# One scan and one product by C over both channel blocks of a step, and all pairs summed by TensorE

## The chip, the cores and the metric

One Trainium2 chip, one core of it. The metric is the device time of one execution in microseconds (us). The engines are called PE (TensorE), DVE (VectorE), ACT (ScalarE), POOL (GpSimd) and SP (SyncE, which issues the DMAs). SBUF is the on-chip memory; PSUM is the accumulator memory, here eight banks of 512 fp32 columns over 128 partitions.

## The reference

A decoder layer on 2048 tokens of 256 channels: layer norm and a Mamba block with its feed-forward part, then cross attention, then a mixture of experts. The change lies in the Mamba block's selective scan, for 512 channels d and 16 states n:

```
def step(h, inp):
    d_t, u_t, b_t, c_t = inp
    dA = jnp.exp(d_t[..., None] * A)
    h = dA * h + (d_t * u_t)[..., None] * b_t[:, None, :]
    y = jnp.einsum('bdn,bn->bd', h, c_t)
    return (h, y)
```

d_t is the step size (a softplus), u_t the channel's input, b_t and c_t come from a projection of u. A is minus the exponential of a weight, so every decay dA lies between 0 and 1. The sequence is one of 2048 steps of time.

## The kernel before

The time axis is cut into four chunks (`NC`) of 512 columns. The 512 channels are four blocks of 128 partitions, taken two at a time: half p = 0 holds blocks 0 and 1, half 1 holds blocks 2 and 3 (`DP` = 2 blocks). A **step** w is one chunk, one half and one state n: 32 steps a chunk (`NU`), 128 in all (`NW_ALL`). A step's work:

- ACT, `decays`: two exponentials of 128x512 into two PSUM banks (2, 3 for even w, 4, 5 for odd w), x = 0 and x = 1. The banks come free when step w - 2 is done with them.
- POOL, `scan_input`: `dbu` = `du` times B, 128x1024, into a ring of three buffers (`DR`), ahead of DVE.
- DVE, `scan` (L864), once for each block x: the recurrence along 512 columns, in place in PSUM, started from the block's column of `carry`. `times_c` (L875), once for each block: the states times C into `hs`, a ring of six. `carry_over` (L882): the last column of both blocks, a 128x2 copy, for the next chunk.
- PE, `add_states`: an identity matmul of 128x512 for each block and state, which sums the states in PSUM banks 0 and 1. An fp32 matmul of 512 columns is two records in the trace. Two steps make a pair j. For the pairs in `SUMMED` (15 of the 64, every fourth but the last) POOL adds the two states first (`add_pair`, L437), and PE sums one state.
- SP, `load_b` and `load_c`: rows of B and C for two steps, broadcast to 128 partitions, two buffers each.

The order of each engine is written out by hand. DVE's loop is

```
for w in range(NW_ALL):
    scan(w, 0)
    if w >= 1:
        times_c(w - 1, 1)
    between(w // NU, w % NU)
    scan(w, 1)
    times_c(w, 0)
    carry_over(w)
```

so that between a scan and its own product another scan stands. `between` (L930 to L988) holds the side work of the neighbouring chunks at a given step i of the chunk: the convolution of the next chunk (steps 9 to 12), the step sizes (`step_rounded` to `step_channels`, steps 6 to 9 and 24 to 28), the gate of the finished half (`gated`, L890, steps 3 and 19), the residuals (`first_residual`, L895; `second_residual`, L911, at step 2 of chunks 2 and 3) and the norms. ACT and PE have their side work at given steps too: ACT the step projection's softplus (steps 4, 5, 22, 23), SiLU (14, 16) and GELU (24, 26, 28, 30); PE the projections, `hidden` (23 to 29) and `ffn_out` (30, 31 and the next chunk's 0, 1). PE's `skip` (L1306) opens the sum of a half and waits for DVE's gate of the half before. The functions of ACT change the activation table: exponential, logarithm, SiLU and GELU each load their own, copies none.

All sharing is by semaphores. A function that waits for its own engine's semaphore waits until the earlier instruction has written.

## Time and profile before

| | |
|---|---|
| median of 3 runs | 1638.37 us (1637.38 to 1647.46) |
| profiled execution: span | 1636.5 us |
| median less that span | 1.9 us |
| busy: PE, DVE, ACT, POOL | 1336.6, 797.4, 904.6, 402.9 us |
| first and last scan start at | 49.7 and 659.4 us |

The span runs from the first to the last instruction of one profiled execution, the only figure that the page gives for that execution. What lies around it in a timed run is of the size of the third line. An engine's busy time is a sum over stages: DVE is busy nearly throughout up to about 660 us, PE and ACT more after it.

### The profile page before, as it was taken

The page shows a single profiled execution, that of the slowest core. Times are in us where ns is not written, and L with a number is a line of the kernel's source. Part 1 is how long each engine was busy: PE and PEld are TensorE (multiplying, and loading weights), DVE is VectorE, ACT ScalarE, POOL GpSimd, SP SyncE. Part 2 cuts the span into 40 slices and gives each one's busy share as a digit, 9 for nine tenths or more (in the row PEclk, how much of TensorE's full clock was granted, in tenths as well). Part 3 has the DMA queues.
Part 4 walks back from the last instruction along what each step waited for, and adds up shares of the span by engine and source line. Part 5 has one row for each costly group of instructions (what it writes and reads, how often), then busy time and mean ns, then how long its engine had stood idle before and what let it go on. Part 6 is the DMA issues. An engine that isn't in the chain of part 4 may idle for free.

```text
span 1636.5 us, 15496 instructions
## 1 busy us (share of the span) xinstructions
PE 1336.6 (82%) x5511; PEld 628.7 (38%) x5511; DVE 797.4 (49%) x1213; ACT 904.6 (55%) x1164; POOL 402.9 (25%) x177
## 2 busy tenths in 40 slices
PE   6477566887598748896735999999999988979999
PEld 2122123343334324653521223223223234568887
DVE  3899989989998899216520002001011016461011
ACT  3536444654466436122435997998998944751310
POOL 0637655654455466015030000000000001000000
PEclk9588787999789878998756999999999988989999
DMA  5323332332243233102994000000000000011701
GB/s 184 118 78 129 129 115 86 122 116 77 82 138 116 77 128 116 45 8 49 102 112 39 1 1 1 1 1 0 0 0 0 0 0 1 1 52 35 325 14 39
DMA packets 35633, 107.96 MB, mean 66 GB/s; under 512 B 3650, under 2 KB 14146, under 8 KB 32915
## 3 DMA queue, kind: packets, MB, share of 16 engines
q1 hardware_dynamic: 35572, 107.19, 23.7%
q8 instruction: 34, 0.56, 0.1%
q14 instruction: 27, 0.22, 0.1%
HBM read 93.60 MB, written 2.36 MB: 59 GB/s over the span
## 4 chain that ended last, share of the span: by engine, by line
PE 47%; DVE 24%; ACT 13%; issue 8%; DMA 5%; SPq 1%; POOL 1%; DVEq 0%; ACTq 0%; POOLq 0%
DVE ps L864 13%; PE ps L1558 10%; PE ps L1543 9%; ACT arena L706 6%; PE ps L1362 4%; PE ps L1667 4%; DMA arena<-arena 4%; PE ps L1708 3%; PE ps L1317 3%; DVE arena L875 2%; PE ps L1685 2%; PE ps L1696 2%; PE ps L1248 2%; SPq L377 1%; PE ps L1588 1%
## 5 line engine op out<-in xcount | busy, mean ns | idle before, releaser
L706 ACT ACTIVATE arena<-ps,bound 128x1024 f32<-128x1024 f32 (+1 forms) x416 | 421.1, 1215 | 26.7 <-PE ps L1543 26.7
L431 POOL TENSOR_TENSOR arena<-arena 128x1024 f32<-128x1024 f32 x128 | 300.7, 2353 | 262.0 <-DVE ps L864 218.1
L864 DVE TENSOR_TENSOR_SCAN ps<-ps,arena 128x512 f32<-128x512 f32 x256 | 327.3, 1279 | 18.1 <-ACT ps L567 13.7
L1317 PE MATMUL ps<-arena,ident 128*128 128x512 f32 x452 | 245.1, 683 | 106.1 <-POOL arena L437 66.1
L567 ACT ACTIVATE ps<-arena 128x512 f32<-128x512 f32 x256 | 173.1, 689 | 269.1 <-DVE arena L882 175.5
L1543 PE MATMUL ps<-arena 97*128 (+3 forms) x832 | 218.9, 385 | 22.8 <-issue 20.7
L1558 PE MATMUL ps<-arena 128*32 128x512 f32 (+1 forms) x1664 | 222.8, 607 | 1.1 <-ACT arena L706 0.9
L1317 PEld LDWEIGHTS ps<-arena,ident 128*128 128x128 f32 x452 | 91.5, 214 | 243.3 <-issue 89.0
L1141 DVE COPY arena<-ps 128x512 f32<-128x512 f32 x16 | 11.1, 691 | 355.8 <-PE ps L1558 355.8
L419 POOL TENSOR_TENSOR rstd<-ve,mhalf 128x4 f32<-128x4 f32 (+3 forms) x18 | 23.5, 1308 | 625.0 <-DVE ve L1166 469.9
L875 DVE TENSOR_TENSOR arena<-ps,arena 128x512 f32<-128x512 f32 x256 | 171.4, 669 | 0.0
L1543 PEld LDWEIGHTS ps<-arena 97*128 97x128 bf16 (+1 forms) x832 | 67.5, 99 | 227.0 <-ACT arena L706 140.6
L1248 PE MATMUL ps<-ident,arena 128*128 128x128 f32 x392 | 58.7, 291 | 40.4 <-DVE arena L1051 13.7
L1248 PEld LDWEIGHTS ps<-ident,arena 128*128 128x128 f32 x392 | 45.1, 147 | 76.0 <-issue 57.5
L1362 PE MATMUL ps<-arena 128*128 128x256 f32 x256 | 62.5, 400 | 12.1 <-ACT arena L583 12.1
L1558 PEld LDWEIGHTS ps<-arena 128*32 128x32 f32 (+1 forms) x1664 | 32.9, 108 | 95.5 <-ACT arena L706 78.3
L1262 PE MATMUL ps<-arena 128*128 128x512 f32 x128 | 62.9, 639 | 4.1 <-DVE arena L895 2.4
L1353 PE MATMUL ps<-arena 128*128 128x512 f32 x128 | 59.9, 615 | 5.5 <-ACT arena L583 4.8
L1667 PE MATMUL ps<-arena 128*128 128x257 f32 x256 | 58.6, 393 | 2.5 <-ACT arena L752 2.5
L1362 PEld LDWEIGHTS ps<-arena 128*128 128x128 f32 x256 | 50.0, 199 | 26.8 <-ACT arena L583 15.4
L1632 PE MATMUL ps<-arena 128*128 128x512 f32 x128 | 59.6, 609 | 0.0
L1708 PE MATMUL ps<-arena 128*128 128x256 f32 x256 | 55.5, 379 | 0.0
(178 smaller groups left out, 1386.5 us busy)
## 6 DMA issues: line engine op xcount, KB each, us to landing
arena<-bc_scratch SPq DMA_DIRECT2D x128, 512.0 KB, 3.7
arena<-in_mw SPq DMA_DIRECT2D x16, 1024.0 KB, 8.7
arena<-arena SPq DMA_DIRECT2D x48, 128.0 KB, 14.8
arena<-arena SPq DMA_DIRECT2D x12, 400.2 KB, 16.4
arena<-in_w SPq DMA_DIRECT2D x2, 1024.0 KB
out<-xt SPq DMA_DIRECT2D x4, 512.0 KB, 2.9
xt<-in_x SPq DMA_DIRECT2D x1, 1536.0 KB
arena<-in_ctx SPq DMA_DIRECT2D x1, 1200.8 KB, 7.8
```

Source lines behind the costliest of these rows:

```text
L431: pool.tensor_tensor(dbu[:, w % DR], du[:, DP * p:DP * p + DP], over(bg[:, w // BG % 2, n % BG], DP), ALU.mult).then_inc(S["dbu_ready"], 1)
L567: act.activation(decay_bank(w, x), delta[:, d], ACT.Exp, scale=neg_a[:, d, n:n + 1]).then_inc(S["da_ready"], 1)
L706: act.activation(flat(prob[0:n, v % 2, 2 * h:2 * h + 2]), ps[0:n, 2 * (r % 3):2 * (r % 3) + 2, :].rearrange("p a b -> p (a b)"), ACT.Exp, ...
L864: dve.tensor_tensor_scan(decay_bank(w, x), decay_bank(w, x), dbu[:, w % DR, x], carry[:, d, n:n + 1], ALU.mult, ALU.add).then_inc(S["scan_ ...
L875: dve.tensor_tensor(state(w)[:, x], decay_bank(w, x), cg[:, w // BG % 2, n % BG], ALU.mult).then_inc(S["hc_ready"], 1)
L1248: return pe.transpose(dst, src, ident[:, :])
L1317: last = mm(bank(x), ident[:, :], state(2 * j + s)[:, x], start=False, stop=(j % HP == HP - 1 and (j in SUMMED or s == 1)))
L1362: mm(acc, gate[:, f, tok(i)], w2[:, f], start=(f == 0), stop=False)
L1543: last = mm(ps[0:n, 2 * (r % 3) + x, :], kx[0:XR + 1, head, b * P:b * P + n], qx[0:XR + 1, head, c * C:c * C + C] if first else qx[0:XR + ...
L1558: last = mm(ps[2 * HD * x:2 * HD * x + 2 * HD, 6 + g % 2, :], vx[0:n, b, G * g + x, :], prob[0:n, v % 2, x], start=(b == 0), stop=(b == KB ...
L1667: last = mm(ps[:, 4 + x if x < 4 else x - 4, 0:DM + 1], lg[:, t, tok(x)], xn[:, t, :], start=(t == 0), stop=(t == TT - 1))
L1708: last = mm(ps[:, t % 8, 0:DM], cwt[:, x, tok(t)], eo[:, x], start=(x == 0), stop=(x == NE - 1))
```

## The change

- `scan` runs once a step over both blocks, 128x1024: it starts from block x = 0's carry. At block 1's first column the decay is made zero, so that nothing of block 0 passes into it: `step_heads` sets the first column of block 1's step sizes to 1e28 (`CUT`) after the true values have been used, and A is kept at most -1e-26 (`LEAST`), so that the exponential of their product is zero. What block 1 should have had from its own carry, its true first decay times its carry, is worked out ahead for all 16 states: `head_decays` on ACT and `step_heads` on DVE give `handed`, and POOL adds its column to `dbu` in an instruction of one column (`scan_input`), after a wait for its own product.
- `times_c` runs once a step, 128x1024, right behind `between`; where `between` is empty, right behind the step's scan. `carry_over` moves to ACT, before the decays that overwrite the banks; it is left out in the last chunk, but the wait for the product stays.
- `SUMMED` is empty: POOL adds no pair, and PE sums both states of every pair.
- The semaphores count accordingly: one scan and one product a step, two for `dbu`, five for the softplus.

```diff
@@ -57,7 +59,7 @@
-SUMMED = [j for j in range(NC * NP - 2) if j % 4 == 2]
+SUMMED = []
...
@@ -173,6 +175,8 @@
+        first_decay = m.take(2, NS)
+        handed = m.take(2, NS)
...
@@ -326,14 +333,14 @@
                 if q >= 2:
-                    sp.wait_ge(S["dbu_ready"], BG * (q - 1))
+                    sp.wait_ge(S["dbu_ready"], 2 * BG * (q - 1))
                 c, n = q // NS, q % HP * BG
...
                 if q >= 2:
-                    sp.wait_ge(S["hc_ready"], DP * BG * (q - 1))
+                    sp.wait_ge(S["hc_ready"], BG * (q - 1))
                 c, n = q // NS, NS + q % HP * BG
...
@@ -424,16 +431,20 @@
                     pool.wait_ge(S["du_ready"], c * DP + p + 1)
+                    pool.wait_ge(S["head_ready"], 2 * (c * DP + p) + 1)
                 if n % BG == 0:
...
                 if w >= DR:
-                    pool.wait_ge(S["scan_done"], DP * (w - DR + 1))
+                    pool.wait_ge(S["scan_done"], w - DR + 1)
                 pool.tensor_tensor(dbu[:, w % DR], du[:, DP * p:DP * p + DP], over(bg[:, w // BG % 2, n % BG], DP),
                                    ALU.mult).then_inc(S["dbu_ready"], 1)
+                pool.wait_ge(S["dbu_ready"], 2 * w + 1)
+                pool.tensor_tensor(dbu[:, w % DR, 1, 0:1], dbu[:, w % DR, 1, 0:1], handed[:, p, n:n + 1],
+                                   ALU.add).then_inc(S["dbu_ready"], 1)
...
-                pool.wait_ge(S["hc_ready"], DP * (2 * j + 2))
+                pool.wait_ge(S["hc_ready"], 2 * j + 2)
                 pool.tensor_tensor(state(2 * j), state(2 * j), state(2 * j + 1), ALU.add).then_inc(S["pair_ready"], 1)
...
@@ -546,24 +557,41 @@
                 h = c * DP + p
-                act.wait_ge(S["sp_act"], h * 4 + 2)
+                act.wait_ge(S["sp_act"], h * 5 + 2)
                 act.activation(flat(sp_exp), flat(sp_exp), ACT.Exp, scale=-1.0).then_inc(S["sp_act"], 1)
...
                 h = c * DP + p
-                act.wait_ge(S["sp_act"], h * 4 + 3)
+                act.wait_ge(S["sp_act"], h * 5 + 3)
                 act.activation(flat(sp_ln), flat(sp_exp), ACT.Ln, bias=1.0).then_inc(S["sp_act"], 1)
+
+            def head_decays(c, p):
+                h = c * DP + p
+                act.wait_ge(S["delta_ready"], h + 1)
+                if h >= 2:
+                    act.wait_ge(S["head_ready"], 2 * (h - 1))
+                act.activation(first_decay[:, p], neg_a[:, DP * p + 1], ACT.Exp,
+                               scale=delta[:, DP * p + 1, 0:1]).then_inc(S["sp_act"], 1)
+
+            def carry_over(w):
+                c, p, n = step(w)
+                act.wait_ge(S["hc_ready"], w + 1)
+                if c + 1 < NC:
+                    if n == 0 and c:
+                        act.wait_ge(S["head_ready"], 2 * (c * DP + p) + 2)
+                    act.activation(carry[:, DP * p:DP * p + DP, n:n + 1],
+                                   ps[:, 2 + DP * (w % 2):2 + DP * (w % 2) + DP, C - 1:C],
+                                   ACT.Copy).then_inc(S["carry_done"], 1)
+                    act.wait_ge(S["carry_done"], w + 1)
...
                 if n == 0:
-                    act.wait_ge(S["delta_ready"], c * DP + p + 1)
+                    act.wait_ge(S["head_ready"], 2 * (c * DP + p) + 2)
+                if w >= 2:
+                    carry_over(w - 2)
                 for x in range(DP):
                     d = DP * p + x
-                    if w >= 2:
-                        act.wait_ge(S["hc_ready"], DP * (w - 2) + x + 1)
-                        if x == 0:
-                            act.wait_ge(S["carry_done"], w - 1)
                     act.activation(decay_bank(w, x), delta[:, d], ACT.Exp,
...
@@ -615,6 +644,8 @@
+                    if i == 9:
+                        head_decays(c, 1)
...
@@ -636,6 +667,8 @@
+                    if i == 28 and more:
+                        head_decays(c + 1, 0)
...
@@ -766,7 +799,7 @@
-            dve.tensor_scalar(flat(neg_a), flat(neg_a), -1.0, None, ALU.mult).then_inc(S["prep_dve"], 1)
+            dve.tensor_scalar(flat(neg_a), flat(neg_a), -1.0, -LEAST, ALU.mult, ALU.min).then_inc(S["prep_dve"], 1)
...
@@ -848,39 +881,39 @@
                 if c:
-                    dve.wait_ge(S["dbu_ready"], (c - 1) * NU + (p + 1) * NS)
+                    dve.wait_ge(S["dbu_ready"], 2 * ((c - 1) * NU + (p + 1) * NS))
                 dve.tensor_tensor(flat(du[:, DP * p:DP * p + DP]), flat(delta[:, DP * p:DP * p + DP]),
...
-            def scan(w, x):
+            def step_heads(c, p):
+                h = c * DP + p
+                dve.wait_ge(S["sp_act"], h * 5 + 5)
+                if c:
+                    dve.wait_ge(S["carry_done"], (c - 1) * NU + (p + 1) * NS)
+                dve.tensor_tensor(handed[:, p], first_decay[:, p], carry[:, DP * p + 1], ALU.mult).then_inc(S["head_ready"], 1)
+                dve.wait_ge(S["du_ready"], h + 1)
+                dve.memset(delta[:, DP * p + 1, 0:1], CUT).then_inc(S["head_ready"], 1)
+
+            def scan(w):
                 c, p, n = step(w)
-                d = DP * p + x
-                if x == 0:
-                    dve.wait_ge(S["dbu_ready"], w + 1)
-                    if w >= NU:
-                        dve.wait_ge(S["carry_done"], w - NU + 1)
-                dve.wait_ge(S["da_ready"], DP * w + x + 1)
-                dve.tensor_tensor_scan(decay_bank(w, x), decay_bank(w, x), dbu[:, w % DR, x],
-                                       carry[:, d, n:n + 1], ALU.mult, ALU.add).then_inc(S["scan_done"], 1)
-
-            def times_c(w, x):
+                dve.wait_ge(S["dbu_ready"], 2 * (w + 1))
+                if w >= NU:
+                    dve.wait_ge(S["carry_done"], w - NU + 1)
+                dve.wait_ge(S["da_ready"], DP * (w + 1))
+                dve.tensor_tensor_scan(decay_banks(w), decay_banks(w), flat(dbu[:, w % DR]),
+                                       carry[:, DP * p, n:n + 1], ALU.mult, ALU.add).then_inc(S["scan_done"], 1)
+
+            def times_c(w):
                 c, p, n = step(w)
-                if x == 0 and n % BG == 0:
+                if n % BG == 0:
                     dve.wait_ge(c_in[w // BG % 2], 16 * (w // BG // 2 + 1))
-                if x == 0 and w >= 2 * RING:
+                if w >= 2 * RING:
                     dve.wait_ge(S["y_acc"], w // 2 - RING + 1)
-                dve.wait_ge(S["scan_done"], DP * w + x + 1)
-                dve.tensor_tensor(state(w)[:, x], decay_bank(w, x), cg[:, w // BG % 2, n % BG],
-                                  ALU.mult).then_inc(S["hc_ready"], 1)
-
-            def carry_over(w):
-
-                c, p, n = step(w)
-                dve.wait_ge(S["scan_done"], DP * (w + 1))
-                dve.tensor_copy(carry[:, DP * p:DP * p + DP, n:n + 1],
-                                ps[:, 2 + DP * (w % 2):2 + DP * (w % 2) + DP, C - 1:C]).then_inc(S["carry_done"], 1)
+                dve.wait_ge(S["scan_done"], w + 1)
+                dve.tensor_tensor(state(w), ps[:, 2 + DP * (w % 2):2 + DP * (w % 2) + DP, :],
+                                  over(cg[:, w // BG % 2, n % BG], DP), ALU.mult).then_inc(S["hc_ready"], 1)
...
@@ -955,6 +988,8 @@
                     step_channels(c, 1)
+                if i == 10:
+                    step_heads(c, 1)
                 if i in (9, 10, 11, 12) and more:
...
@@ -986,6 +1021,8 @@
                         step_channels(c + 1, 0)
+                    if i == 29:
+                        step_heads(c + 1, 0)
...
@@ -999,16 +1036,12 @@
             step_channels(0, 0)
+            step_heads(0, 0)
             dve.wait_ge(S["w_mamba"], 16 * 6)
             for w in range(NW_ALL):
-                scan(w, 0)
-                if w >= 1:
-                    times_c(w - 1, 1)
+                scan(w)
                 between(w // NU, w % NU)
-                scan(w, 1)
-                times_c(w, 0)
-                carry_over(w)
-            times_c(NW_ALL - 1, 1)
+                times_c(w)
             second_residual(NC - 2)
...
@@ -1312,8 +1345,8 @@
                     for x in range(DP):
-                        if j not in SUMMED:
-                            pe.wait_ge(S["hc_ready"], DP * (2 * j + s) + x + 1)
+                        if x == 0 and j not in SUMMED:
+                            pe.wait_ge(S["hc_ready"], 2 * j + s + 1)
                         last = mm(bank(x), ident[:, :], state(2 * j + s)[:, x], start=False,
```

## Rows read from the trace of the kernel before

**Rows 1.** The page, busy tenths in 40 slices: DVE.

```profile
DVE  3899989989998899216520002001011016461011
```

**Rows 2.** Scan's line: duration ns min/median/max, first and last start us.

```profile
L864 DVE TENSOR_TENSOR_SCAN ps<-ps,arena x256: 1266/1278/1293, 49.7 to 659.4; 128x512 f32<-128x512 f32 x128
```

**Rows 3.** View of waits, 40 to 700 us: total us, times, longest us.

```profile
DVE ps L864 <- ACT ps L567: 13.7, 12, 2.4
...
DVE ps L864 <- POOL arena L431: 4.1, 2, 2.5
```

**Rows 4.** Timeline, DVE: start us, duration us; a step with nothing between.

```profile
575.34 1.28 DVE L864 TENSOR_TENSOR_SCAN ps<-ps,arena 128x512 f32<-128x512 f32 x1
576.53 0.67 DVE L875 TENSOR_TENSOR arena<-ps,arena 128x512 f32<-128x512 f32 x1
577.12 1.27 DVE L864 TENSOR_TENSOR_SCAN ps<-ps,arena 128x512 f32<-128x512 f32 x1
...
578.90 0.14 DVE L882 COPY arena<-ps 128x2 f32<-128x2 f32 x1
578.96 1.28 DVE L864 TENSOR_TENSOR_SCAN ps<-ps,arena 128x512 f32<-128x512 f32 x1
```

**Rows 5.** Timeline, DVE: a 1024-wide product from PSUM and the next instruction.

```profile
538.01 1.21 DVE L890 TENSOR_TENSOR arena<-ps,arena 128x1024 f32<-128x1024 f32 x1
539.14 1.28 DVE L864 TENSOR_TENSOR_SCAN ps<-ps,arena 128x512 f32<-128x512 f32 x1
```

**Rows 6.** Timeline, DVE: two products, the second waiting for the first.

```profile
566.26 1.22 DVE L837 TENSOR_TENSOR arena<-arena 128x1024 f32<-128x1024 f32 x1
567.59 1.22 DVE L844 TENSOR_TENSOR arena<-arena 128x1024 f32<-128x1024 f32 x1
```

**Rows 7.** Groups by line and shape, POOL: count, busy us, mean ns, idle before.

```profile
L431 POOL TENSOR_TENSOR arena<-arena 128x1024 f32<-128x1024 f32 x128 | 300.7, 2353 | 262.0 <-DVE ps L864 218.1 <-DVE arena L852 37.8 <-DMA arena<-bc_scratch 6.0
...
L419 POOL TENSOR_TENSOR rstd<-ve,mhalf 128x4 f32<-128x4 f32 x14 | 14.4, 1032 | 122.2 <-DVE ve L916 81.1 <-DVE ve L900 24.8 <-DVE ve L793 13.2
...
L491 POOL TENSOR_TENSOR bound<-bound,half 128x1 f32<-128x1 f32 x1 | 0.5, 549 | 25.8 <-DVE bound L1102 25.8
```

**Rows 8.** Groups by line and shape, 0 to 680 us: pair sums, decays, table loads.

```profile
L1317 PE MATMUL ps<-arena,ident 128*128 128x512 f32 x451 | 244.7, 683 | 106.1 <-POOL arena L437 66.1 <-DVE arena L875 39.8
L567 ACT ACTIVATE ps<-arena 128x512 f32<-128x512 f32 x256 | 173.1, 689 | 269.1 <-DVE arena L882 175.5 <-DVE arena L875 91.8 <-DVE arena L844 1.3
...
L567 ACT ACT_TABLE_LOAD x25 | 32.1, 1283 | 0.4
```

**Rows 9.** Timeline, chunk 1 from step 5, and step 6 of chunk 2.

```profile
219.57 1.98 PE L1300 MATMUL ps<-arena 16*128 16x512 f32 x4
...
223.92 1.29 DVE L864 TENSOR_TENSOR_SCAN ps<-ps,arena 128x512 f32<-128x512 f32 x1 [2.37 <-ACT ps L567]
...
229.88 1.29 DVE L864 TENSOR_TENSOR_SCAN ps<-ps,arena 128x512 f32<-128x512 f32 x1 [1.64 <-ACT ps L567]
...
386.54 1.29 DVE L864 TENSOR_TENSOR_SCAN ps<-ps,arena 128x512 f32<-128x512 f32 x1 [2.29 <-ACT ps L567]
```

**Rows 10.** Timeline, start of chunk 2: the residual of the feed-forward part.

```profile
369.64 0.69 DVE L911 TENSOR_TENSOR arena<-ps,arena 128x512 f32<-128x512 f32 x1 [7.86 <-PE ps L1364]
```

**Rows 11.** Timeline, the last steps of chunk 3: a decay, and PE's chain.

```profile
655.87 0.69 ACT L567 ACTIVATE ps<-arena 128x512 f32<-128x512 f32 x1 [0.82 <-DVE arena L875]
...
659.20 5.41 PE L1362 MATMUL ps<-arena 128*128 128x256 f32 x16 [2.44 <-ACT arena L583]
```

**Rows 12.** Timeline, chunk 2, steps 14 to 18: the pair sum and what follows.

```profile
439.42 0.67 DVE L875 TENSOR_TENSOR arena<-ps,arena 128x512 f32<-128x512 f32 x1
...
445.94 3.78 PE L1317 MATMUL ps<-arena,ident 128*128 128x512 f32 x4 [7.37 <-POOL arena L437]
...
453.94 3.60 PE L1317 MATMUL ps<-arena,ident 128*128 128x512 f32 x8
...
457.91 1.29 DVE L864 TENSOR_TENSOR_SCAN ps<-ps,arena 128x512 f32<-128x512 f32 x1 [1.78 <-ACT ps L567]
```

More of the change, by code:

```diff
@@ L52 @@
 ENGINES = 4
+CUT = 1e28
+LEAST = 1e-26
 DP = DB // 2
@@ L256, in decoder_layer @@
 mark1 st1 ve1 rs1 a0_ready a0t_ps a0t_ready z_ps u_ps u_raw z_ready hist_in conv_step u_ready
-            xdbl_ps xdbl_ready bc_stored b_even b_odd c_even c_odd dt_ps sp_in sp_act sp_step delta_ready
+            xdbl_ps xdbl_ready bc_stored b_even b_odd c_even c_odd dt_ps head_ready sp_in sp_act sp_step delta_ready
             du_ready da_ready dbu_ready scan_done carry_done hc_ready pair_ready y_acc skip_done
@@ L287, in decay_bank, with decay_banks @@
             return bank(2 + DP * (w % 2) + x)
+        def decay_banks(w):
+            return banks(2 + DP * (w % 2), DP)
         def work(x):
@@ L602, in _ @@
             step_log(0, 0)
+            head_decays(0, 0)
             decays(0)
@@ L824, in step_rounded @@
                 h = c * DP + p
-                dve.wait_ge(S["sp_act"], h * 4 + 3)
+                dve.wait_ge(S["sp_act"], h * 5 + 3)
                 dve.tensor_scalar(flat(sp_cor), flat(sp_exp), 1.0, 1.0, ALU.add, ALU.subtract).then_inc(S["sp_step"], 1)
@@ L834, in step_sum @@
                 h = c * DP + p
-                dve.wait_ge(S["sp_act"], h * 4 + 4)
+                dve.wait_ge(S["sp_act"], h * 5 + 4)
                 dve.wait_ge(S["sp_step"], h * 3 + 2)
```

## The prediction

> **What bounds the kernel now.** I read the page's slices first. VectorE (DVE) is at 8 to 9 tenths in the first sixteen slices of about 41 us and seldom above 2 in the middle of the kernel [rows 1], so the scan stage is DVE's and the later stages are not. The change touches only the scan stage. Next, the view of the scan's line: 256 scans from 49.7 to 659.4 us [rows 2], that is 128 steps of two. The view of waits then says why DVE is not full in there: its scans wait 13.7 us for ScalarE's (ACT's) exponentials, in twelve places, and 4.1 us for POOL [rows 3]; where two chunks meet, the residual of L911 waits for PE, 7.86 us at the start of chunk 2 [rows 10]. So DVE sets the time, with a few places where ACT or PE does. Last, the timeline, for what a step costs from start to start. That is not an instruction's duration, as neighbours overlap: a step with nothing between takes 578.96-575.34 = 3.62 us: two scans of 1.19, two products of 0.59, and 0.06 for the carry copy [rows 4].
>
> **The change on DVE, per step.** Three things are saved.
> Product: a 1024-wide product from PSUM takes 539.14-538.01 = 1.13 us [rows 5] against 2 x 0.59: 0.055 saved.
> Carry copy, moved to ACT: 0.06 saved.
> Scan: no 1024-wide scan is in the trace. The bounds are nothing saved, and the whole that does not scale. If the scan had the product's fixed part, 2 x 0.59 - 1.13 = 0.055, the saving would be that. If instead each column costs the scan twice what it costs the product, 512 columns take 2 x (1.13-0.59) = 1.08 us and 0.12 of the 1.19 is fixed. I take 0.125, because a recurrence at a whole multiple of the product's pace is the simpler reading, and keep 0 and 0.055 for the range.
> One thing is given back. The product must now follow its own scan, where before another instruction stood between. Its start then loses the 0.08 overlap (0.67 long, 0.59 to the next start [rows 4]) at least; the dependent pair L837, L844 starts 1.33 apart where 1.13 is usual [rows 5, 6], 0.20 at most. I take 0.14. Where the step has side work between scan and product (L930 to L988), this is covered.
> So a covered step gains 0.125 + 0.055 + 0.065 = 0.245 us and a plain one 0.105.
>
> The Trainium skill weighs in on both. Its Vector Engine (DVE) Microarchitecture Reference, Measured stream behaviour on trn2, gives about 75 ns per instruction after overlap, also for programs of several micro-operations. By that figure the scan saves 0.075, as an estimate from that page, and the total below would be 5 us worse; the trace's 1.19 us does not by itself tell the two apart.
>
> **How many steps count.** From `between`, with the two new head steps: 74 steps are covered (21, 20, 20 and 13 in the four chunks) and 54 plain. A gain is lost where DVE waits afterwards for something that did not get faster: steps 3 to 7 of chunk 1 and 3 to 5 of chunks 2 and 3 (ACT, below), the five steps before L911 in chunks 2 and 3 (PE), and the last two. That leaves 65 covered and 40 plain: 65 x 0.245 + 40 x 0.105 = 20.1 us.
>
> **What is added.**
> (a) Head steps, eight times a 128x16 product and a memset on DVE: the 128x2 copy lasts 0.14 [rows 4], so about 0.2 a pair with its wait, **+1.6**. The ACT heads are eight short exponentials beside other work: nothing, or 8 x 0.69 at most if ACT were the bound.
> (b) POOL's one-column add. Bounds: POOL's 128x1 power took 0.55 and the 128x4 one 1.03 [rows 7]; below, near nothing. I take 0.45. A POOL round is then 2.35 + 0.05 + 0.45 = 2.85 us against DVE's 3.4 or more, so it is hidden by the three buffers of `dbu`. It shows where POOL starts cold: at the first scan +0.6, and after the root at step 2 of chunk 0, where POOL waits for DVE and DVE for POOL, +1.0. **+1.6**. Without that cover 128 times 0.45 would be 58 us.
> (c) ACT per step. Before, the first decay was due at a step's start and the second 1.8 us later. Now both and the carry copy are due at the start. The copy: between 0.14, as on DVE, and the 0.69 of an exponential [rows 4, 8]; with the wait on itself I take 0.35. What ACT may do beside the decays between two steps shrinks from about 4.0 to 3.55 us. The twelve waits of 13.7 us in all are where it did more. Four of them (2.37 at step 6 of chunk 1, with 1.64 behind it, and 2.29 at step 6 of chunk 2, which chunk 3 repeats) come by a chain: DVE's gate at step 3, PE's skip and two pairs, the step projection L1300, four ACT operations, decays [rows 9]. In it the gate comes 0.48 later in its step (behind a whole scan), then the second exponential and the copy: 0.48 + 0.6 + 0.3, so the scan is later by 1.3 to 1.4 in each chunk: **+4.0**. Of the other eight one is (e)'s, and seven share what is left, 13.7 - 2.37 - 1.64 - 2 x 2.29 - 1.78 = 3.3 us, 0.5 each; they grow by as much again, +3.5, and some places just clear before will show, +1.3: **+4.8**.
> (d) PE has 15 pairs more to sum in full: 30 matmuls, 60 records of 0.684 us, 41 us of PE [rows 8]. They lie beside DVE's work; what they cost on the path is at the boundary of two chunks, where one such pair (j = 14 of the chunk) stands in PE's chain before L911's wait [rows 10]: +1.85 for 4 records at 0.46 (8 of them take 3.60 where PE had not just been idle, 4 took 3.78 after its long wait [rows 12]). ACT starts that chain 0.8 sooner, having no second wait between its two exponentials (0.82 there [rows 11]), and less of step 2 is left behind the residual, -0.7. Twice +0.35: **+0.7**.
> (e) POOL's pair adds go. PE waited 7.37 us for one in chunk 2, then did the gates late, ACT's SiLU late, and the scan waited 1.78 us [rows 12]. Its products start at 439.42 and last 0.67, so now PE sums the pair 5.8 us sooner, if twice as long: **-1.8**. Elsewhere such waits of PE had no one behind them.
> (f) The stage's end is PE's chain from ACT's last GELU [rows 11]; it starts 0.8 sooner in its step: **-0.8**. The pairs in that chain were never POOL's.
> DMA: `load_b` and `load_c` keep their place and their two steps of lead; nothing waits behind them.
>
> Sum: -20.1 + 1.6 + 1.6 + 4.0 + 4.8 + 0.7 - 1.8 - 0.8 = **-10.0 us**. The profiled execution spans 1636.5 us, 1.9 below the median of 1638.37, so I forecast 1626.5 in span and **1628 us** as time.
>
> **Rivals.**
> *A, the scan saves nothing by being long.* For it: no row shows another length. Then 105 x 0.125 = 13.1 us go and the time is 1641, no change.
> *B, ACT keeps up.* If (c) costs nothing and the dependent product no more than an independent one (40 x 0.14 = 5.6), 8.8 + 5.6 = 14.4 more is gained: 1614. For it: ACT idles 269 us before its decays [rows 8]. Against: 13.7 us of waits exist already. The Trainium skill's page VectorE: DVE Perf Modes, The DRAIN you can't avoid, says that a semaphore between neighbours costs nothing extra; by that the 5.6 would be gained. L837 and L844 in rows 5 and 6 speak against it.
> *C, slower: ACT becomes the pacer.* Its place is the scan of each step after a group of ACT work that changes the table (GELU, logarithm, SiLU): the exponential table is brought back 25 times, at 1.28 us [rows 8]. If the ring of two banks has no slack left there, each costs the second exponential 0.69, the copy with its wait 0.4 and the later side work 0.48, 1.6 us: 25 x 1.6 = 40 in place of 8.8, 1659. It decides from about 1.4 us a group ((16.4 + 10 + 8.8) / 25). Against: between those groups DVE has side work in most steps.
> That POOL paces would need an add of over 1.1 us, above every row of its size.
>
> **Chances.** What a measurement can tell from no change is about 1%, 16.4 us. Forecast 55% (1618 to 1638, a tenth of it past 1%), A 13%, B 20%, C 12%. So faster 0.25, same 0.63, slower 0.12. The range starts at 1612 (B, a little past it) and ends at 1644 (A, with the copy nearer its upper bound); C is left out.
>
> **What would show it.** One scan of 128x1024 with a start-to-start of 2.26 us (2.39 would be A), a dependent product 0.04 to 0.15 after the scan's end, plain steps of 3.5. DVE's waits for the exponentials near 20 us instead of 13.7 (5 is B, over 45 is C). POOL's add near 0.45. PE's 66 us of waits for POOL gone, and L911 waiting about as before. The forecast is wrong if POOL's round exceeds DVE's step or if scans wait for ACT in most steps.

## The result: slower by 2.8%, outside the range

The changed kernel takes 1686.37 us (median of 4 runs, 1683.08 to 1688.74), the kernel before beside it 1638.1: a ratio of 1.0282 [1.0254, 1.031]. The forecast was 1628 us, the range 1612 to 1644. I gave 0.12 to slower, for a rival that was not what happened.

The page after (busy tenths of 40 slices; PEclk is the granted clock of TensorE; the span is 1687.0 us, 50.5 longer than before's 1636.5):

```profile
span 1687.0 us, 15369 instructions
...
DVE  3899989996999799512722001001001015561001
...
PEclk9679887899879987969765999999999987989999
```

DVE is as full in the scan stage as in [rows 1]. The stage only lasts longer. Its groups (line, engine, operation, out<-in x count, then busy us, mean ns of one, idle before and its releasers), against [rows 2, 3, 7, 8]:

```profile
L439 POOL TENSOR_TENSOR arena<-arena 128x1024 f32<-128x1024 f32 x128 | 327.1, 2556 | 236.7 <-DVE ps L904 190.0
L1350 PE MATMUL ps<-arena,ident 128*128 128x512 f32 x512 | 261.0, 651 | 67.1 <-DVE arena L915 67.0
L904 DVE TENSOR_TENSOR_SCAN ps<-ps,arena 128x1024 f32<-128x1024 f32 x128 | 300.7, 2350 | 25.7 <-ACT ps L595 15.5
...
L595 ACT ACTIVATE ps<-arena 128x512 f32<-128x512 f32 x256 | 166.3, 682 | 71.1 <-DVE arena L915 67.2
...
L915 DVE TENSOR_TENSOR arena<-ps,arena 128x1024 f32<-128x1024 f32 x128 | 156.0, 1219 | 7.0 <-DVE ps L904 0.5
...
L582 ACT ACTIVATE arena<-ps 128x2 f32<-128x2 f32 x96 | 16.5, 172 | 215.4 <-DVE arena L915 215.4
```

Nearly everything that the forecast priced is there at its price: one scan of 2350 ns, products of 1219, waits for ACT of 15.5 us (and 4.8 for the carry copy), no wait of PE for POOL. Two things are not. POOL's multiply is longer, 2556 ns against 2353. And the work in `between`, whose lines the change doesn't touch, is much longer on DVE. Before and then after, in the view of DVE's groups (L816 is now L849, L905 is L938, L812 is L845, L844 is L877):

```profile
L816 DVE SCALAR_TENSOR_TENSOR arena<-arena,chan 128x512 f32<-128x512 f32 x48 | 36.1, 752 | 1.7
...
L844 DVE TENSOR_TENSOR arena<-arena 128x1024 f32<-128x1024 f32 x8 | 9.8, 1219 | 0.5
...
L905 DVE SCALAR_TENSOR_TENSOR arena<-arena,rstd,scales 128x256 f32<-128x256 f32 x16 | 9.1, 629 | 1.2 <-POOL rstd L419 1.2
L812 DVE TENSOR_SCALAR arena<-arena,chan 128x512 f32<-128x512 f32 x16 | 8.6, 537 | 6.6 <-ACT arena L517 6.6
```

```profile
L849 DVE SCALAR_TENSOR_TENSOR arena<-arena,chan 128x512 f32<-128x512 f32 x48 | 49.8, 1038 | 1.7
...
L845 DVE TENSOR_SCALAR arena<-arena,chan 128x512 f32<-128x512 f32 x16 | 18.9, 1184 | 6.6 <-ACT arena L528 6.6
...
L877 DVE TENSOR_TENSOR arena<-arena 128x1024 f32<-128x1024 f32 x8 | 17.6, 2195 | 0.5
L938 DVE SCALAR_TENSOR_TENSOR arena<-arena,rstd,scales 128x256 f32<-128x256 f32 x16 | 13.1, 880 | 1.2 <-POOL rstd L426 1.2
```

The timeline tells why (start us, duration us). First before, two steps of the convolution in chunk 0:

```profile
102.20 0.53 DVE L812 TENSOR_SCALAR arena<-arena,chan 128x512 f32<-128x512 f32 x1
...
102.77 2.32 DVE L816 SCALAR_TENSOR_TENSOR arena<-arena,chan 128x512 f32<-128x512 f32 x3
105.01 1.29 DVE L864 TENSOR_TENSOR_SCAN ps<-ps,arena 128x512 f32<-128x512 f32 x1
106.20 0.67 DVE L875 TENSOR_TENSOR arena<-ps,arena 128x512 f32<-128x512 f32 x1
106.37 2.35 POOL L431 TENSOR_TENSOR arena<-arena 128x1024 f32<-128x1024 f32 x1 [4.03 <-DVE ps L864]
```

POOL's multiply is released by a step's second scan. Behind it DVE has a product, the carry copy, a scan and a product, all with an operand in PSUM, and only then side work. They take 0.59 + 0.06 + 1.19 + 0.59 = 2.43 us [rows 4]; POOL's 2.35 all but fit in: it ends at 108.72, the side work starts at 108.63. The same work after:

```profile
105.72 2.35 DVE L904 TENSOR_TENSOR_SCAN ps<-ps,arena 128x1024 f32<-128x1024 f32 x1
...
107.98 0.16 DVE L893 TENSOR_TENSOR arena<-arena 128x16 f32<-128x16 f32 x1
108.05 2.72 DVE L845 TENSOR_SCALAR arena<-arena,chan 128x512 f32<-128x512 f32 x1
...
108.15 2.34 POOL L439 TENSOR_TENSOR arena<-arena 128x1024 f32<-128x1024 f32 x1 [5.80 <-DVE ps L904]
110.57 0.25 POOL L442 TENSOR_TENSOR arena<-arena 128x1 f32<-128x1 f32 x1
110.81 2.32 DVE L849 SCALAR_TENSOR_TENSOR arena<-arena,chan 128x512 f32<-128x512 f32 x3
...
116.44 0.52 DVE L845 TENSOR_SCALAR arena<-arena,chan 128x512 f32<-128x512 f32 x1
116.68 2.48 POOL L439 TENSOR_TENSOR arena<-arena 128x1024 f32<-128x1024 f32 x1 [5.86 <-DVE ps L904]
117.00 4.29 DVE L849 SCALAR_TENSOR_TENSOR arena<-arena,chan 128x512 f32<-128x512 f32 x3
```

The end of the scan now releases two things at once: POOL's multiply, and DVE's side work. An instruction of 0.53 us becomes one of 2.72, and ends just after POOL's multiply does (110.77 against 110.49). Three that took 2.32 take 4.29. Later in the stage DVE wins the race, and POOL pays; where the side work reads PSUM, neither does:

```profile
607.97 1.20 DVE L885 TENSOR_TENSOR arena<-arena 128x1024 f32<-128x1024 f32 x1
608.20 3.17 POOL L439 TENSOR_TENSOR arena<-arena 128x1024 f32<-128x1024 f32 x1 [3.50 <-DVE ps L904]
...
619.69 0.67 DVE L928 TENSOR_TENSOR arena<-ps,arena 128x512 f32<-128x512 f32 x1
619.86 2.36 POOL L439 TENSOR_TENSOR arena<-arena 128x1024 f32<-128x1024 f32 x1 [0.90 <-DVE ps L904]
```

So the two engines exclude each other when both work from SBUF alone: one waits, with its instruction started, until the other's is over. The Trainium skill has this rule (SBUF — State Buffer, Who interferes with whom): DVE's second read port is also GpSimd's only one, and "A DVE instruction with two SBUF inputs contends with a GpSimd instruction that reads SBUF"; the one that has the port keeps it for the whole instruction, and a `tensor_scalar` contends too when it runs in a fast mode that uses both ports. The rows agree. L845, a `tensor_scalar`, reads one tensor from SBUF and waits all the same; that it runs in such a mode no row shows by itself. It was the page that spoke against this change, and I did not weigh it.

### The profile page after: what moved, and what is told of

Its sections match the earlier page's. It is cut to its first block, busy times and chain, and to the rows that moved or that the text cites. A ratio compares the mean times of both kernels' runs of the same rounds, so it can differ in the third digit from the quotient of the medians.

```text
span 1687.0 us, 15369 instructions
## 1 busy us (share of the span) xinstructions
PE 1370.0 (81%) x5571; PEld 646.2 (38%) x5571; DVE 815.6 (48%) x845; ACT 914.2 (54%) x1268; POOL 424.0 (25%) x290
## 4 chain that ended last, share of the span: by engine, by line
PE 46%; DVE 24%; ACT 15%; issue 8%; DMA 5%; SPq 2%; POOL 0%; DVEq 0%; ACTq 0%; POOLq 0%
DVE ps L904 11%; PE ps L1591 9%; PE ps L1576 9%; ACT arena L739 6%; PE ps L1395 4%; PE ps L1700 3%; DVE arena L915 3%; DMA arena<-arena 3%; PE ps L1741 3%; PE ps L1350 3%; DVE arena L849 2%; ACT ps L595 2%; PE ps L1718 2%; PE ps L1281 2%; PE ps L1729 2%
## 5 line engine op out<-in xcount | busy, mean ns | idle before, releaser
L439 POOL TENSOR_TENSOR arena<-arena 128x1024 f32<-128x1024 f32 x128 | 327.1, 2556 | 236.7 <-DVE ps L904 190.0
L1350 PE MATMUL ps<-arena,ident 128*128 128x512 f32 x512 | 261.0, 651 | 67.1 <-DVE arena L915 67.0
L904 DVE TENSOR_TENSOR_SCAN ps<-ps,arena 128x1024 f32<-128x1024 f32 x128 | 300.7, 2350 | 25.7 <-ACT ps L595 15.5
L595 ACT ACTIVATE ps<-arena 128x512 f32<-128x512 f32 x256 | 166.3, 682 | 71.1 <-DVE arena L915 67.2
L1350 PEld LDWEIGHTS ps<-arena,ident 128*128 128x128 f32 x512 | 100.5, 205 | 213.2 <-issue 113.2
L915 DVE TENSOR_TENSOR arena<-ps,arena 128x1024 f32<-128x1024 f32 x128 | 156.0, 1219 | 7.0 <-DVE ps L904 0.5
L582 ACT ACTIVATE arena<-ps 128x2 f32<-128x2 f32 x96 | 16.5, 172 | 215.4 <-DVE arena L915 215.4
L1281 PE MATMUL ps<-ident,arena 128*128 128x128 f32 x392 | 62.6, 303 | 42.5 <-DVE arena L1084 13.7
L1295 PE MATMUL ps<-arena 128*128 128x512 f32 x128 | 68.9, 689 | 21.8 <-DVE arena L928 12.0
L1395 PE MATMUL ps<-arena 128*128 128x256 f32 x256 | 66.3, 417 | 14.8 <-ACT arena L611 14.8
L1339 PE MATMUL ps<-arena 128*128 128x512 f32 x32 | 25.4, 937 | 60.3 <-DVE arena L923 60.3
L1386 PE MATMUL ps<-arena 128*128 128x512 f32 x128 | 60.2, 618 | 5.1 <-ACT arena L611 4.4
## 6 DMA issues: line engine op xcount, KB each, us to landing
arena<-arena SPq DMA_DIRECT2D x48, 128.0 KB, 15.1
```

Of the source, the lines that this page charges most:

```text
L439: pool.tensor_tensor(dbu[:, w % DR], du[:, DP * p:DP * p + DP], over(bg[:, w // BG % 2, n % BG], DP), ALU.mult).then_inc(S["dbu_ready"], 1)
L595: act.activation(decay_bank(w, x), delta[:, d], ACT.Exp, scale=neg_a[:, d, n:n + 1]).then_inc(S["da_ready"], 1)
L904: dve.tensor_tensor_scan(decay_banks(w), decay_banks(w), flat(dbu[:, w % DR]), carry[:, DP * p, n:n + 1], ALU.mult, ALU.add).then_inc(S["s ...
L915: dve.tensor_tensor(state(w), ps[:, 2 + DP * (w % 2):2 + DP * (w % 2) + DP, :], over(cg[:, w // BG % 2, n % BG], DP), ALU.mult).then_inc(S ...
L1281: return pe.transpose(dst, src, ident[:, :])
L1295: last = mm(dst, win[:, k, tok(o)], a0t[:, k], start=(k == 0), stop=(k == DK - 1))
```

## The experiments

The first four ask which part of the change costs the time. The kernel before took 1637.27 us (median) beside them.

**e1: POOL released later.** In the changed kernel, the multiply waits for the product of the step instead of its scan.

```
-                    pool.wait_ge(S["scan_done"], w - DR + 1)
+                    pool.wait_ge(S["hc_ready"], w - DR + 1)
```

> The changed kernel, with one edit: POOL's multiply for step w waits for the product by C of step w-3 instead of for its scan. Theory 1 (DVE and POOL block each other: the multiply is now released just when DVE's side work starts): the multiply starts with DVE's next scan, the mean of the side work returns to the durations of before (L845 from 1.18 to 0.54 us, L849 from 1.04 to 0.75, L877 from 2.2 to 1.22), POOL's multiply from 2.56 to 2.35, and the time falls by 35 to 50 us from 1686, to 1636 to 1651. Theory 2 (ACT is the pacer: both decays and the copy are due at the step's start): the time stays within 5 us of 1686. Theory 3 (PE is the pacer, with 41 us of sums more): also within 5 us of 1686.

Measured: 1640.99 us (1639.27 to 1644.88), ratio 1.0015 [0.9999, 1.0031]. Of the 48 us (1686.37 - 1638.1), 45 are gone by one wait that comes later. The groups are back at their length:

```profile
L904 DVE TENSOR_TENSOR_SCAN ps<-ps,arena 128x1024 f32<-128x1024 f32 x128 | 300.6, 2349 | 26.2 <-ACT ps L595 16.0 <-POOL arena L442 5.4 <-ACT arena L582 4.8
...
L849 DVE SCALAR_TENSOR_TENSOR arena<-arena,chan 128x512 f32<-128x512 f32 x48 | 36.1, 752 | 1.7
...
L877 DVE TENSOR_TENSOR arena<-arena 128x1024 f32<-128x1024 f32 x8 | 10.1, 1265 | 0.5
...
L845 DVE TENSOR_SCALAR arena<-arena,chan 128x512 f32<-128x512 f32 x16 | 8.8, 549 | 6.6 <-ACT arena L528 6.6
```

The view by windows has the sum. Its columns are the stretch, its length, then busy us of PE, PEld, DVE, ACT and POOL, the granted clock, the DMA share and GB/s. First the changed kernel, then e1, each from 50 us to its last gate (the last of DVE's eight products of L890, now L923; with it the scan stage ends):

```profile
50.00:722.00 672.00, 484.62 (x1144) 224.83 (x1144) 598.17 (x445) 323.53 (x565) 363.02 (x262) 0.86 0.29 98
```

```profile
50.00:678.00 628.00, 481.25 (x1144) 225.62 (x1144) 553.18 (x445) 323.88 (x567) 345.98 (x262) 0.87 0.31 105
```

The same 445 instructions keep DVE busy 598.17 and 553.18 us: 45.0 more, all of the difference of the stretches (44).

**e2: all pairs summed by PE, nothing else.** The kernel before with `SUMMED = []`.

> The kernel before, with SUMMED empty and nothing else changed: POOL adds no pair, PE sums both states of all 64 pairs. Theory 1: PE's 41 us lie beside DVE's work, 1635 to 1643. Theory 3 (PE): most of the 48 us of the change shows here already, 1660 or more.

Measured: 1636.41 us (1626.26 to 1646.53), ratio 1.0013 [0.9997, 1.0029]. In the median nothing, but its runs spread over 20 us. The profiled one, of 1626.26, has its last gate at 673.5 us, against 685.6 before. That part of the change costs nothing and shortens the stage by 12 us. Its other runs have no trace. e6 is the same kernel with three matmuls more; ten of its eleven runs lie within 5.3 us.

**e3: the side work moved behind the second scan of the kernel before.** No merged scan, no merged product.

```
-                between(w // NU, w % NU)
                 scan(w, 1)
+                between(w // NU, w % NU)
```

> The kernel before, with the call of between moved from in front of the step's second scan to behind it; scans, products, copies and sums as before. POOL's multiply is then released right when the side work starts. Theory 1: the side work with two SBUF inputs takes 30 to 45 us longer in sum, and the time is 1665 to 1685. Theories 2 and 3: no decay is due sooner and PE has nothing more to do, 1636 to 1645.

Measured: 1687.25 us (1686.98 to 1691.39), ratio 1.0307 [1.0289, 1.0324]. A loss as large, made in the old kernel by a change of order alone. That the two totals agree is chance: here the last gate comes at 737.9 us, 52.3 later than before, and 47 of these are DVE's longer busy time; behind it the clock stays, and the stretch to the first key projection takes 68.0 us as before. The changed kernel's last gate comes 36.3 later (721.9), and the rest of its loss stands behind it, as said below. The rows of e3:

```profile
L816 DVE SCALAR_TENSOR_TENSOR arena<-arena,chan 128x512 f32<-128x512 f32 x48 | 53.7, 1119 | 1.7
...
L844 DVE TENSOR_TENSOR arena<-arena 128x1024 f32<-128x1024 f32 x8 | 17.5, 2194 | 0.5
```

**e4: the changed kernel with POOL's 15 pair adds back** (`SUMMED` as before).

> The changed kernel, with POOL adding the 15 pairs again as before. Theory 1: no help, as POOL has 15 more instructions that read SBUF, 1683 to 1700. Theory 3 (PE): the time falls by 20 us or more. Theory 2: within 5 us of 1686.

Measured: 1682.9 us (1676.76 to 1689.56), ratio 1.027 [1.0229, 1.0311]. PE's additional sums are no cause.

One thing was left. In e1 the last gate starts at 677.5 us, 8.1 before that of the kernel before, and yet e1 is no faster: from there to the first key projection it takes 81.1 us (677.5 to 758.6), the kernel before 68.0 (685.6 to 753.6). None of this code is touched. The windows of the value projection, before and then e1:

```profile
691.00:697.00 6.00, 4.76 (x23) 3.84 (x21) 1.90 (x4) 1.39 (x7) 0.00 (x0) 1.00 0.87 223
697.00:707.00 10.00, 9.69 (x35) 5.71 (x36) 4.04 (x9) 0.43 (x3) 7.06 (x3) 1.00 0.00 0
```

```profile
683.00:690.00 7.00, 4.69 (x23) 3.79 (x21) 2.96 (x6) 1.82 (x8) 0.00 (x0) 0.98 0.71 181
690.00:700.00 10.00, 10.00 (x19) 5.50 (x20) 2.97 (x6) 0.00 (x0) 7.05 (x3) 0.50 0.00 0
```

And its first matmuls in the timeline, before and then e1:

```profile
697.31 1.13 PE L1432 MATMUL ps<-arena 96*128 96x256 f32 x4 [1.55 <-DMA arena<-in_wo]
```

```profile
689.98 2.08 PE L1465 MATMUL ps<-arena 96*128 96x256 f32 x4 [2.31 <-DMA arena<-in_wo]
```

PE waits 2.31 us for the attention weights instead of 1.55, and then runs at a granted clock of 0.50 (1.2 GHz) where before it had 1.00 (2.4 GHz): 19 records in 10 us instead of 35. The changed kernel is much the same there (721.9 to 803.2, 81.3 us; the wait is 2.62 us). But e2's profiled run waited as long as e1 and kept its clock, so the length of the wait alone doesn't decide:

```profile
686.06 1.13 PE L1432 MATMUL ps<-arena 96*128 96x256 f32 x4 [2.38 <-DMA arena<-in_wo]
```

The next four put three identity matmuls, whose result nothing reads, in front of that wait, so that PE is not idle in it. The kernel before took 1638.39 us beside them.

```
+            for _ in range(3):
+                mm(bank(5), ident[:, :], win[:, 0, 0:512], start=True, stop=True)
             pe.wait_ge(S["w_attn"], 16 * 5)
             values(0, VE)
```

**e5: e1 with the filler.**

> The changed kernel with the late release, and three more matmuls of 128x512 on PE into a free bank, between the last out projection and the wait for the attention weights; their result is not used. In the traces of the changed kernel and of its late-release form PE waited 2.3 to 2.6 us there, and the value projection behind ran with matmuls at half pace for some 25 us (0.82 as mean granted clock of the tail). Theory 1a (the clock falls in that wait and this costs the merged kernels 13 us that their scan stage does not cause): no half-pace matmuls in the tail, 1625 to 1633. Theory 1b (the tail's length has another cause): 1638 to 1646, as without the matmuls.

Measured: 1629.99 us (1628.68 to 1631.96), ratio 0.9944 [0.9922, 0.9966]. The tail takes 69.0 us (676.3 to 745.3).

**e6: e2 with the filler.**

> The kernel before with SUMMED empty (PE sums all pairs), and the same three matmuls. Its profiled run without them took 1626.3 us with a full clock in the tail, its other runs 1635 to 1647. Theory 1a: runs near 1626, 1622 to 1630, and this is the fastest kernel so far, as the removed pair adds no longer block DVE's side work. Theory 1b: 1634 to 1642 as without them.

Measured: 1627.12 us (1625.38 to 1645.7), ratio 0.9944 [0.992, 0.9968]: faster than both kernels by a little, with the lowest median of those that do all of the work, and it has neither the merged scan nor the merged product. From e5 the times don't tell it apart (the ratios are the same). The traced run is its fastest; its last gate comes at 673.7 us. Its rows, against before's L905 above and [rows 3]:

```profile
L864 DVE TENSOR_TENSOR_SCAN ps<-ps,arena 128x512 f32<-128x512 f32 x256 | 327.9, 1281 | 13.8 <-ACT ps L567 9.4 <-POOL arena L431 4.1
...
L921 DVE SCALAR_TENSOR_TENSOR arena<-arena,rstd,scales 128x256 f32<-128x256 f32 x16 | 6.7, 477 | 1.1 <-POOL rstd L419 1.1
L905 DVE SCALAR_TENSOR_TENSOR arena<-arena,rstd,scales 128x256 f32<-128x256 f32 x16 | 6.7, 478 | 1.2 <-POOL rstd L419 1.2
```

L905 falls from 629 to 478 ns, L921 from 738 to 477, with POOL's pair adds gone: the kernel before paid for the same exclusion already. At 388.93 us its four of L921 take 3.76 us, beside a pair add that starts at 388.49; at 451.80 its four of L905 take 2.48, beside a multiply that had to queue behind a pair add. Those are (151 + 261) x 16 ns = 6.6 us of side work, and the scans' waits for ACT fall by 4.3.

**e7: the kernel before with the filler.**

> The kernel before with the same three matmuls. Its trace had a full clock in the tail already. Theory 1a: within 3 us of before, 1634 to 1641. Theory 1b: the same.

Measured: 1647.72 us (1639.87 to 1650.14), ratio 1.0035 [1.0014, 1.0055]. It had nothing to win there, and loses; 1634 to 1641 was expected. Its runs stand in two groups, five from 1639.87 to 1641.56 and six from 1647.72 to 1650.14. The traced one (1648.7) is of the upper group: the clock falls later, at 743 us, after stretches in which PE was busy for 21.07 of 22 us (as it was before, where the clock stayed):

```profile
720.00:742.00 22.00, 21.07 (x85) 14.67 (x83) 1.55 (x3) 3.19 (x10) 0.00 (x0) 1.00 0.00 0
743.00:760.00 17.00, 16.84 (x33) 8.23 (x32) 9.75 (x39) 1.91 (x4) 7.13 (x3) 0.50 0.18 63
```

**e8: the changed kernel with the filler.**

> The changed kernel as it is, with the same three matmuls. Theory 1a: 13 us less, 1670 to 1677, so that what is left of the loss against before is the port's: some 36 us in the scan stage. Theory 1b: 1683 to 1689.

Measured: 1671.38 us (1668.68 to 1673.6), ratio 1.0197 [1.017, 1.0223]; the tail is 68.9 us. So the changed kernel's 48 us are two things: 33 to e8 (1671.38 - 1638.39), which stand in the scan stage, and 15 from e8 to the changed kernel, most of it TensorE's clock in a stage that the change doesn't touch. In the traces the tail is 12.4 us shorter (81.3 and 68.9). The last gates of the two differ as well, 721.9 and 716.3, though nothing up to there was edited: a last gate of one trace is good to some us only.

The last four ask what the merge itself is worth. The kernel before took 1637.08 us beside them.

**e9: e5 without POOL's one-column add** (left out: the column that carries a state over the seam for the second block).

> The changed kernel with late release and filler matmuls, without POOL's one-column add: what block 1 should take over from the chunk before is left out of the computation. Theory 1 (the port): the add is at most 0.3 us long and holds up the first piece of side work of a covered step by as much, so 3 to 12 us less than 1630. Theory 4 (what the merge saves is given back by ACT, which must deliver both decays and the copy at the start of a step): within 3 us of 1630.

Measured: 1631.22 us (1629.88 to 1634.45), ratio 0.9962 [0.9948, 0.9976]. The add costs nothing that can be told.

**e10: e6 with the side work behind the second scan, and POOL released later still.** The order of e3, without its collision.

```
-                between(w // NU, w % NU)
                 scan(w, 1)
+                between(w // NU, w % NU)
...
                     pool.wait_ge(S["scan_done"], DP * (w - DR + 1))
+                    pool.wait_ge(S["hc_ready"], DP * (w - DR) + 1)
```

> The kernel before with PE summing all pairs, filler matmuls, the side work behind the second scan (where it cost 50 us), and POOL's multiply released by the first product by C of step w-3 instead of by its second scan. Theory 1: the multiply lies wholly beside scans and products again, the side work has its short durations, and the 50 us are gone: 1622 to 1632. If the place of the side work itself cost them: 1670 or more.

Measured: 1640.92 us (1636.37 to 1649.47), ratio 1.0017 [0.9994, 1.004], where e3 took 1687.25 (e3 has POOL's pair adds and no filler besides). L844 takes 1218 ns again (L845 in its numbering), so the collision is gone; the forecast of 1622 to 1632 is missed all the same. Over e6 it is 14 us. In the traces the last gate comes 16.0 later (689.7; the traced run took 1646.03), and most of that is in the scans' waits, 27.1 us instead of 13.8:

```profile
L865 DVE TENSOR_TENSOR_SCAN ps<-ps,arena 128x512 f32<-128x512 f32 x256 | 328.2, 1282 | 27.1 <-ACT ps L568 19.2 <-POOL arena L432 7.7
```

**e11 and e12: e5 and e6 with light ACT work** (left out: GELU and SiLU, in whose place stands Relu, so no table is changed for them).

> The changed kernel with late release and filler, with Relu in place of GELU and SiLU in the Mamba part, so that ACT has 19 pairs of table loads less (the functions are left out of the computation). Theory 4: the scans' waits for ACT fall from 21 us to under 8 and the kernel gains more by it than the unmerged one: at least 8 us faster than its unmerged partner in this call, near 1605. Otherwise (the merge saves nothing on DVE): level with its partner.

> The partner: the kernel before with PE summing all pairs and filler, with Relu in place of GELU and SiLU (left out of the computation as well). Its scans waited 9 us for ACT. Theory 4: 1612 to 1622, slower than the merged one by 8 us or more. Otherwise level with it.

Measured: 1624.18 us (1622.52 to 1625.37), ratio 0.9913 [0.9881, 0.9944], and 1624.91 (1622.4 to 1627.05), ratio 0.9913 [0.9881, 0.9946]. The two are level in time, four runs each, as e5 and e6 nearly are, and the merged one's scans still wait 15.1 us for the exponentials and 4.4 for the copy, against 10.0. So it isn't the work with tables that they wait for. But the stage's end speaks for a part of it: the merged kernel's last gate moves from 676.3 (e5) to 669.9 us (e11), the other's stays at 673.7 (e6, e12), and up to it the residual's waits for PE fall from 42.7 to 36.8 us in the merged kernel and not in the other (39.9 and 41.1). How much of what the merge gives back comes from GELU and SiLU stays open. The longest of these waits in e5 stand where they stood in [rows 9], 3.78 us (at 223.03), 1.95 (229.05) and 2.22 (384.27): behind the gate, PE's sums and the step projection.

## Why the prediction was wrong, step by step

**The step that failed.** In "What is added" I wrote that POOL's round of 2.85 us "is hidden by the three buffers of `dbu`", and costed the side work, which I had only moved, at its old durations. Both took POOL and DVE as free of each other but for semaphores. But the change moves `between` from in front of the step's last scan to behind it, and that scan's end is POOL's release (190.0 us of POOL's idle time end there, in 92 of 128 multiplies). The rivals had ACT or POOL as pacers; none had two engines in each other's way. In the changed kernel the same instructions keep DVE busy for 598.17 us instead of 553.18 (e1), and POOL's multiply takes 2556 ns instead of 2353. e1 and e5 against the changed kernel and e8 show the size in time, 45 and 41 us; e3 shows that the order alone does it, and e10 that the same order without the collision doesn't. The prediction's test "the forecast is wrong if POOL's round exceeds DVE's step" looked at the right engine and the wrong quantity.

The trace of before held the evidence, in the view of one line (duration ns min/median/max). I had read means only:

```profile
L905 DVE SCALAR_TENSOR_TENSOR arena<-arena,rstd,scales x16: 467/472/2148, 288.4 to 701.8; 128x256 f32<-128x256 f32 x16
```

**A second loss, not in any step**, is the clock in the tail, 12 to 15 us. Before, that stretch had 1.00; I let the stage's end shift by some us and the rest of the kernel stay as it was.

**The terms that were priced**, measured in e5, where neither of the two stands much in the way:

```profile
585.94 2.35 DVE L904 TENSOR_TENSOR_SCAN ps<-ps,arena 128x1024 f32<-128x1024 f32 x1
...
588.39 1.23 DVE L915 TENSOR_TENSOR arena<-ps,arena 128x1024 f32<-128x1024 f32 x1
589.53 2.35 DVE L904 TENSOR_TENSOR_SCAN ps<-ps,arena 128x1024 f32<-128x1024 f32 x1
```

- Scan: 107.98 - 105.72 = 2.26 us from start to start with other work behind it, as forecast; 2 x 1.19 - 2.26 = 0.12 saved. Rival A (2.39) falls, and so does 0.075, the estimate that the prediction made from the Trainium skill (Vector Engine (DVE) Microarchitecture Reference, Measured stream behaviour on trn2).
- A product behind its own scan starts 588.39 - 585.94 = 2.45 us after it: 0.19 lost, where I took 0.14 of at most 0.20. A plain step is 589.53 - 585.94 = 3.59 us, against 3.62 in [rows 4]: 0.03 saved instead of 0.105. On 40 steps that is 3 us less. This step is one of the better: over the 43 plain steps of e5's timeline the medians are 2.47 and 3.61, so the product loses 0.21, more than the bound of 0.20, and the merge saves next to nothing there. So rival B's 5.6 us, which took a dependent product to cost no more than another, fall too.
- (a) The head product takes 0.30 us in the mean instead of the 0.14 of the copy, 0.21 and 0.28 to the next start in two places (at 188.04 and 101.75): about +2 (forecast +1.6). And `between` with the head steps covers 75 steps, not 74 (21 in chunk 1), which is 0.1 us.
- (b) POOL's add: 0.25 us instead of 0.45, and its waits 5.4 instead of 4.1 [rows 3], +1.3 (forecast +1.6).
- (c) ACT: 15.6 + 4.8 = 20.4 us of waits in e5. The forecast was 13.7 + 8.8 = 22.5. Right in size. But without the pair adds and without the merge (e6) it is 9.4, so the merge costs 11.0 here, more than the 8.8.
- (d) The residual of the feed-forward part waits 42.7 us up to the last gate in e5 and 38.2 before: +4.5, forecast +0.7. PE's additional sums, which (d) was about, are in e6 as well, with 39.9: +1.7. The other 2.8 come with the merge.
- (e) PE sums the pairs: -1.8 forecast. The last gate of e6 comes 11.9 us earlier than before (673.7 and 685.6). I saw PE's wait for POOL and not what POOL's adds did to DVE.
- (f) From the start of the last step to the last gate it is 27.97 us before (657.60 to 685.57) and 27.79 in e5 (648.55 to 676.34): -0.2, forecast -0.8.

For the stage the sum was -10.0, and e5's last gate is 9.3 earlier than before (676.3). That looks like a hit and isn't one: of these, 11.9 belong to (e), and the merge of scan and product is worth 676.3 - 673.7 = 2.6 us in the wrong direction. That is no more than two traces of one stage can differ by, so it says that the merge gains nothing, not that it loses. Its terms give about that: 65 x 0.23 + 40 x 0.03 = 16.2 saved (a covered step is 2.26 + 1.13 = 3.39 instead of 3.62), and 1.6 + 1.3 + 11.0 + 2.8 = 16.7 given back. About 3 us more go to what is left of the exclusion in e5: POOL's multiply starts 0.16 to 0.23 us behind a scan and lasts 2.35, the side work starts 2.26 behind the scan, and L885 takes 1344 ns where its like in e6 takes 1221.

**Open** stays what makes the granted clock fall. That the filler removes the fall in the tail is shown for e5 against e1 and for e8 against the changed kernel. For e6 it isn't: e2's only trace has no such fall. That e2 kept its clock behind a wait of 2.38 us, and that e7 lost it with PE nearly always busy, shows that the wait for the weights isn't the whole cause. No run separates the rest.

## What to carry to other kernels

When an edit moves DVE work, look at what POOL runs at the place it moves to: instructions of both that work from SBUF alone exclude each other for their whole length, and no wait in the profile names it; it shows as the same line and shape with two durations (467 and 2148 ns above). A release is a start time: if the instruction that frees a buffer is also the last one before such work, move the release behind an instruction with an operand in PSUM. And compare min, median and max of a group before its mean serves as a price.

## What the runs showed of the hardware

- While one of the two waits for the other, its instruction is booked as running: 2.72 us for one of 0.53 (DVE), 3.17 for one of 2.35 (POOL). Either can be the one that waits, and the booked starts don't tell which: L845, booked from 108.05, waited for a multiply booked from 108.15, and at 607.97 and 608.20 it was the multiply that waited.
- The scan runs at 2.09 ns a column, (2350 - 1279) / 512, half the pace of the product ((1219 - 669) / 512 = 1.07), also over a seam between two PSUM banks.
- A stage that ends 8 us earlier can leave the kernel no faster (e1, ratio 1.0015): the granted clock behind it was 0.50 instead of 1.00 for long enough to cost 13 us. Three matmuls of no use brought 11 us back (e5 against e1).
